# A selective-scan block kernel: GpSimd makes six of sixteen drive units, the opening is cut in halves, and the last sum is taken in HBM

## The chip, the cores and the metric

The kernel runs on one NeuronCore of a Trainium2 chip. The metric is the device time of one execution in microseconds (us), the median of several runs; lower is better. One execution was also recorded by the hardware profiler, and all rows below come from that one.

## What is computed

For 16 sequences of 256 tokens with 128 features the reference computes two residual blocks:

```python
x = x + layernorm(block(layernorm(x)))          # block: a gated selective scan (state space model)
x = x + layernorm(ffn(layernorm(x)))            # ffn: both operands rounded to fp8 e4m3, one 128x128 product, bias
# inside block, with 256 inner channels and 16 states each:
xz = x @ W_in + b_in; x_in, z = split(xz)
xc = silu(causal_conv4(x_in) + conv_b)
B, C = split(xc @ W_xp + b_xp); delta = softplus(xc @ W_dt + b_dt)
h[t] = exp(delta[t] * A) * h[t-1] + (delta[t] * xc[t]) * B[t]      # per channel and state
y = sum over states of h * C + D_skip * xc
out = (y * silu(z)) @ W_out + b_out; returns norm(x + out) * alpha + beta
```

The second term of the recurrence, delta * xc * B, is called the drive here, and delta * xc is `u`.

## The kernel before, in words

**Tiling.** Sequences are worked on in eight pairs. In a pair the 256 channels are two halves of 128 partitions, and the 16 states are eight groups of two (`SG = 2`). A unit is one group of one sequence of the pair, so a pair has sixteen units, numbered n = 2 * group + sequence, and each unit has two scans (one per half of the channels) of 128 partitions by 512 elements: two states of 256 steps.

**A unit's way.** The drive of a unit is made by TensorE (PE) in `drive_unit`: `uT`, the transposed `u`, is multiplied by `diag`, a matrix that has B on its diagonal, so that PSUM then holds u times B for two states (four matmuls in the program for a unit, eight records in the trace). `diag` is made by GpSimd (POOL) in `diag_b` with one affine select (L500), and there are four buffers of it. ScalarE (ACT) makes `decay`, exp(delta * A), in `exp_decay` (L745). VectorE (DVE) runs the scan in `scan_half` (L1200), with decay from SBUF and the drive from PSUM. PE transposes the states back (L1011), and they are scaled by C and summed over the groups: for five groups ACT scales (L766) and a DMA issued by POOL adds the result up in SBUF (`add_terms`, L516), for the groups in `DIRECT = (3, 6, 7)` DVE does both (`add_direct`, L1223).

**Slots.** The work is software-pipelined by hand. In slot p the sixteen units of pair p run; beside them the front of pair p+1 (projections, silu, softplus, `u`, B and C) and the back of pair p-1 (sum of the states in `sum_states` L525 and L527, gate, output product, three norms). Every engine runs `slot()` over its own list of instructions in order. The dictionaries `POOL_STEPS`, `ACT_STEPS`, `PE_STEPS` and `DVE_STEPS` say after which step of a slot a piece of front or back work is issued; POOL and DVE count two steps per unit, PE and ACT three. `LEAD = 3` says how many units POOL's `diag` is ahead. The drive has two PSUM buffers of two banks, the states have four buffers. Slots 1 to 6 are a loop; slot 0 has no back, slot 7 no front.

**Opening.** Before slot 0 the front of pair 0 is done in a line: load, layer norm, transposition (L924), `w_tap` = W_in times the convolution weights (L1397), input product (L938 to L943), bias into `pre` (L688) and then silu (L696), the delta product (L954), softplus as exp and log (L722, L726), `delta` (L1189), `u` on POOL (L488), its transposition (L978) and copy (L731), and the first drive.

**Tail.** After slot 7 comes the back of pair 7, then the largest absolute value of all, then the ffn for eight groups of 512 tokens: ACT scales (L864), DVE and POOL round to fp8 (L1462, L1465, L626, L1473), PE multiplies (L1140, L1144), DVE takes statistics (L1482), ACT normalizes into `fn` (L872), POOL adds the residual `x_all` into `fo` (`last_sum`, L633), and the SP queue stores it (L449).

**Queues.** SP issues the loads in a fixed order at the start (L424 to L443) and only the eight stores at the end. POOL issues the 64 accumulating DMAs.

## Time and profile before

| What | us |
|---|---|
| median of 3 runs (lowest, highest) | 639.04 (636.86, 639.94) |
| the profiled execution | 639.14 |
| its span, from the first record to the last | 637.4 |
| PE busy | 542.6 (85%) |
| DVE busy | 504.8 (79%) |
| ACT busy | 441.9 (69%) |
| POOL busy | 300.7 (47%) |

The profiled execution took 1.74 us more than its span. The stretches that the prediction speaks of are: opening 0 to 43.6, slot 0 43.6 to 108.3, slots 1 to 6 up to 505.0 (the one at 240.7 to 306.3 is shown), slot 7 up to 566.5, the back of the last pair up to 593.8, and the tail to 637.4. A busy share is a mean over all of these, and the engine with the largest share need not set the pace in each.

### The profile page before, as it was taken

The page shows a single profiled execution, that of the slowest core. Times are in us where ns is not written, and L with a number is a line of the kernel's source. Part 1 is how long each engine was busy: PE and PEld are TensorE (multiplying, and loading weights), DVE is VectorE, ACT ScalarE, POOL GpSimd, SP SyncE. Part 2 cuts the span into 40 slices and gives each one's busy share as a digit, 9 for nine tenths or more (in the row PEclk, how much of TensorE's full clock was granted, in tenths as well). Part 3 has the DMA queues.
Part 4 walks back from the last instruction along what each step waited for, and adds up shares of the span by engine and source line. Part 5 has one row for each costly group of instructions (what it writes and reads, how often), then busy time and mean ns, then how long its engine had stood idle before and what let it go on. Part 6 is the DMA issues. An engine that isn't in the chain of part 4 may idle for free. (4 is left out here: it accounts for less than half of the span.)

```text
span 637.4 us, 10358 instructions
## 1 busy us (share of the span) xinstructions
PE 542.6 (85%) x2893; PEld 419.1 (66%) x2893; DVE 504.8 (79%) x1001; ACT 441.9 (69%) x885; POOL 300.7 (47%) x333
## 2 busy tenths in 40 slices
PE   4979899999899988998999899998999797861571
PEld 3557687787678866876687767786778686660120
DVE  4036698979887988799979878888989989974695
ACT  2466985799659874989498938894799586702364
POOL 2042343656455563458255826373647465401374
PEclk9979999999899999999999999999999999977555
DMA  7000535053502460155115420624052506510012
GB/s 209 22 1 1 100 67 100 1 100 66 101 2 55 79 134 1 33 99 107 25 33 99 87 47 9 123 46 86 1 112 54 99 10 124 106 27 0 1 51 82
DMA packets 19184, 39.84 MB, mean 62 GB/s; under 512 B 3648, under 2 KB 9920, under 8 KB 19136
## 3 DMA queue, kind: packets, MB, share of 16 engines
q0 software_dynamic: 9216, 33.56, 26.7%
q1 hardware_dynamic: 9920, 5.78, 3.3%
q14 instruction: 35, 0.29, 0.1%
q8 instruction: 13, 0.21, 0.1%
HBM read 3.68 MB, written 2.10 MB: 9 GB/s over the span
## 5 line engine op out<-in xcount | busy, mean ns | idle before, releaser
L1200 DVE TENSOR_TENSOR_SCAN state<-decay,drive 128x512 f32<-128x512 f32 x256 | 297.2, 1203 | 30.7 <-PE drive L995 24.9
L995 PE MATMUL drive<-diag,uT 128*128 128x256 f32 x1024 | 245.9, 384 | 0.7 <-ACT uT L731 0.7
L745 ACT ACTIVATE decay<-delta,a_neg 128x510 f32<-128x510 f32 x256 | 170.5, 730 | 54.8 <-DVE state L1200 53.9
L995 PEld LDWEIGHTS drive<-diag,uT 128*128 128x128 f32 x1024 | 187.1, 193 | 21.7 <-ACT uT L731 1.0
L1011 PE MATMUL hT<-ident,state 128*128 128x128 f32 x1024 | 143.0, 278 | 24.3 <-DVE acc_d L1223 19.1
L1011 PEld LDWEIGHTS hT<-ident,state 128*128 128x128 f32 x1024 | 119.8, 143 | 56.3 <-issue 26.1
L500 POOL TENSOR_SCALAR_AFFINE_SELECT diag<-Bt 128x512 f32<-128x512 f32 x128 | 92.1, 725 | 74.5 <-PE drive L995 58.2
L766 ACT ACTIVATE term<-hT,Ct 128x256 f32<-128x256 f32 x256 | 102.9, 484 | 8.8 <-PE hT L1011 8.8
L516 POOL DMA_DIRECT2D acc<-term x64 | 59.9, 935 | 24.1 <-DMA acc<-term 11.8
L1223 DVE SCALAR_TENSOR_TENSOR acc_d<-hT,Ct,acc_d 128x256 f32<-128x256 f32 x160 | 66.5, 470 | 4.4 <-PE hT L1011 4.3
L938 PE MATMUL fbank<-xnT,w_tap 128*128 128x512 f32 x112 | 50.4, 592 | 0.0
L552 POOL TENSOR_TENSOR bstd<-bvar,half 128x4 f32<-128x4 f32 x8 | 8.3, 1032 | 62.3 <-DVE bvar L1270 62.3
L938 PEld LDWEIGHTS fbank<-xnT,w_tap 128*128 128x128 f32 x112 | 21.5, 192 | 21.1 <-issue 20.2
L472 POOL TENSOR_TENSOR rstd<-var,minus_half 128x4 f32<-128x4 f32 x9 | 9.3, 1031 | 52.8 <-DVE var L1161 52.8
L656 ACT ACTIVATE nrm<-res,bshift,bscale 128x128 f32<-128x128 f32 x32 | 13.1, 481 | 25.9 <-DVE bshift L1254 25.9
L954 PE MATMUL fbank<-xc,w_dt 128*128 128x512 f32 x60 | 28.3, 594 | 0.7 <-ACT xc L696 0.7
L766 ACT ACTIVATE acc<-hT,Ct 128x256 f32<-128x256 f32 x64 | 25.1, 485 | 4.0 <-PE hT L1011 4.0
L552 POOL TENSOR_TENSOR bstd<-bvar,minus_half 128x4 f32<-128x4 f32 x16 | 16.5, 1029 | 24.2 <-DVE bvar L1292 14.9
L525 POOL TENSOR_TENSOR ysumT<-acc 128x512 f32<-128x512 f32 x14 | 17.8, 1270 | 20.8 <-DVE acc_d L1223 20.8
L688 ACT ACTIVATE pre<-fbank,in_bias 128x512 f32<-128x512 f32 x14 | 9.6, 688 | 23.5 <-PE fbank L941 23.5
L532 POOL TENSOR_TENSOR yv<-yv,sz 128x1024 f32<-128x1024 f32 x7 | 16.5, 2360 | 15.2 <-DVE yv L1229 15.2
L488 POOL TENSOR_TENSOR u<-delta,xc 128x1024 f32<-128x1024 f32 x8 | 18.8, 2350 | 7.8 <-DVE delta L1189 7.8
(170 smaller groups left out, 624.9 us busy)
## 6 DMA issues: line engine op xcount, KB each, us to landing
acc<-term POOLq DMA_DIRECT2D x64, 512.0 KB, 4.5
out_dram<-state SPq DMA_DIRECT2D x8, 256.0 KB, 2.2
x_all<-in_L_attn_x_dram SPq DMA_DIRECT2D x2, 256.0 KB, 4.2
state<-in_L_attn_conv_w_dram SPq DMA_DIRECT2D x1, 512.0 KB, 5.4
w_in<-in_L_attn_W_in_dram SPq DMA_DIRECT2D x1, 256.0 KB, 3.2
w_dt<-in_L_attn_W_dt_dram SPq DMA_DIRECT2D x1, 256.0 KB, 5.1
w_out<-in_L_attn_W_out_dram SPq DMA_DIRECT2D x1, 128.0 KB, 3.8
w_ffn<-in_L_ffn_weight_dram SPq DMA_DIRECT2D x1, 64.0 KB, 2.4
```

What stands on the lines that cost most here:

```text
L488: nc.gpsimd.tensor_tensor(u[:, :, :], d, xc[:, par, :, :], ALU.mult).then_inc(u_ready, 1)
L500: nc.gpsimd.affine_select(out=diag[:, n % DIAGS, :, :, :].rearrange("p c s t -> p (c s) t"), in_=b_cols, compare_op=ALU.is_equal, fill=0.0 ...
L516: pool.dma_start(acc[:, par, b, :, :, :], term[:, j % TERMS, :, :, :], accum_op=ALU.add)\
L552: nc.gpsimd.tensor_tensor(bstd[:, :], bvar[:, :], (half if k == 0 else minus_half)[:, :], ALU.pow)\
L745: last = nc.scalar.activation(decay[:, g % DECAYS, h, :, s, 1:], delta[:, par, h, :, 1:], ACT.Exp, scale=a_neg[:, h, SG * g + s:SG * g + s ...
L766: last = nc.scalar.activation(into, hT[:, c, DI * s:DI * s + DI], ACT.Copy, scale=Ct[:, par, TC * b + c, SG * g + s:SG * g + s + 1])
L938: nc.tensor.matmul(front_bank(pr, k), w_tap[:, tap, P * k:P * k + P], xnT[:, :, tap:tap + L], start=(tap == 0), stop=False)
L954: last = nc.tensor.matmul(front_bank(pr, 4 + m), w_dt[:, h, P * m:P * m + P], xc[:, par, h, :], start=(h == 0), stop=(h == HALVES - 1))
L995: last = nc.tensor.matmul(dst[:, :, P * c:P * c + P], uT[:, par, TC * b + c, P * h:P * h + P], diag[:, n % DIAGS, c, :, :], start=True, st ...
L1011: last = nc.tensor.transpose(hT[:, c, DI * s + P * h:DI * s + P * h + P], state[:, n % STATES, h, s, P * c:P * c + P], ident[:, :])
L1200: nc.vector.tensor_tensor_scan(state[:, n % STATES, h, :, :].rearrange("p s t -> p (s t)"), decay[:, g % DECAYS, h, b, :, :].rearrange("p ...
L1223: nc.vector.scalar_tensor_tensor(out=a, in0=src, scalar=by, in1=a, op0=ALU.mult, op1=ALU.add)\
```

## The change

**Drive.** For groups `MADE = (1, 3, 5)`, that is units 2, 3, 6, 7, 10 and 11, `drive_unit` and `diag_b` do nothing on PE. Instead POOL multiplies u by B in SBUF (`make_drive`, two instructions of 128x512 per unit) into the buffer `made`, and the scan of these units reads both inputs from SBUF. For this B must stand in all 128 partitions: SP stores B of the three groups to an internal HBM tensor `b_rows`, element by element, and loads each group back as a broadcast row of 4 KB to every partition into `b_all`, which has one buffer, so the load of the second and third group waits until the group before is used up. **Buffers.** `diag` has two buffers instead of four, and LEAD is 2. `pre` shares the space of `dt_v`, and the sum of the states is taken in place in `acc`.

**Places.** Most entries of the step dictionaries move.

**Opening.** `w_tap` is made ahead of the quantization of the ffn weight, with its load issued earlier; silu reads PSUM directly; exp, log, delta and `u` are done in halves; `u` of pair 0 and one of the two copies of `uT` go to DVE; the norm of pair 1 moves ahead on ACT.

**Tail.** SP stores x after the first block (`store_x1`) to the output in each slot, and the normalized ffn result is added to it in HBM by an accumulating DMA that POOL issues. `fn` has four buffers, and `last_sum` and `fo` are gone.

```diff
-LEAD = 3
+LEAD = 2
 DECAY_LEAD = 1
-DECAYS, DIAGS, STATES, TERMS = 2, 4, 4, 4
+DECAYS, DIAGS, STATES, TERMS = 2, 2, 4, 4
...
+MADE = (1, 3, 5)
+DRIVEN_G = tuple(g for g in range(DS // SG) if g not in MADE)
+DRIVEN = PAIR * len(DRIVEN_G)
+MADES = PAIR * HALVES * len(MADE)
...
-POOL_STEPS = dict(front_root=(3,), front_residual=(24,), front_u=(25,), back_gate=(11,), back_affine=(21,),
-                  back_sum=(25,), sum_states=(6,), back_root=(13, 22, 27))
-ACT_STEPS = dict(back_h2T=(47,), front_xin=(8, 9), silu_table=(21,), front_silu=(21, 22, 23), exp_table=(23,),
-                 front_norm=(14,), front_xnT=(23,), front_dt=(29, 30), front_exp=(35,), front_log=(37,),
-                 front_uT=(42, 46), back_norms=(32, 40, 45))
-PE_STEPS = dict(front_in=(0, 6, 15, 21), front_transpose=(23,), front_dt=(24, 28), front_bc=(37,),
-                front_ut=(40, 41), back_y=(12, 14), back_out=(19,), back_transpose=(45,))
-DVE_STEPS = dict(front_stats=(1,), front_shift=(1,), front_low=(19,), front_bc=(25,), front_delta=(24,),
-                 back_y=(8, 9), back_norms=(12, 13, 17, 21, 24, 27, 27), back_amax=(31,))
+POOL_STEPS = dict(front_root=(2,), front_residual=(31,), front_u=(26,), back_gate=(10,), back_affine=(19,),
+                  back_sum=(25,), sum_states=(6,), back_root=(15, 21, 26))
+ACT_STEPS = dict(back_h2T=(46,), front_xin=(6, 9), silu_table=(21,), front_silu=(21, 22, 23), exp_table=(23,),
+                 front_norm=(7,), front_xnT=(23,), front_dt=(27, 30), front_exp=(35,), front_log=(37,),
+                 front_uT=(45, 46), back_norms=(31, 39, 46))
+PE_STEPS = dict(front_in=(0, 6, 12, 21), front_transpose=(23,), front_dt=(24, 28), front_bc=(33,),
+                front_ut=(42, 42), back_y=(13, 15), back_out=(19,), back_transpose=(45,))
+DVE_STEPS = dict(front_stats=(0,), front_shift=(2,), front_low=(19,), front_bc=(23,), front_delta=(23,),
+                 back_y=(8, 9), back_norms=(12, 13, 17, 21, 23, 27, 27), back_amax=(31,))
...
+        b_rows = nc.dram_tensor("b_rows", [len(MADE), PAIR * TC * SG, P], F32, kind="Internal").ap()
+        b_all = sb("b_all", [P, PAIR, TC, SG, P])
+        made = sb("made", [P, PAIR, HALVES, SG, L])
...
+            def spread_b(pr, par):
+                sp.wait_ge(bc_ready, nth(pr, 3, 2))
...
+                for k, g in enumerate(MADE):
...
+                    sp.dma_start(b_rows[k].rearrange("r p -> p r"),
+                                 Bt[:, par, g, :, :, :].rearrange("p b c s -> p (b c s)"), **slow).then_inc(b_stored[k], 16)
+                for k, g in enumerate(MADE):
+                    sp.wait_ge(b_stored[k], nth(pr, 16, 16))
...
+                    if k:
+                        sp.wait_ge(made_ready, nth(pr, MADES, PAIR * HALVES * k))
...
+                    sp.dma_start(b_all[:, :, :, :, :].rearrange("p b c s t -> p (b c s t)"),
+                                 b_rows[k].rearrange("(o r) p -> o (r p)", o=1).to_broadcast([P, SG * TOK]))\
+                        .then_inc(b_spread[k], 16)
...
+            def store_x1(pr):
+                sp.wait_ge(b_sum, nth(pr, 1, 1))
...
+                sp.dma_start(out_v[:, bass.ds(pr.v * CH, CH), :], x_k[:, bass.ds(pr.v * CH, CH), :]).then_inc(x1_stored, 16)
...
+            def make_drive(pr, par, n):
+                g, b = n // PAIR, n % PAIR
+                j, k = turn(MADE, n), MADE.index(g)
+                pool.wait_ge(u_ready, nth(pr, 1, 1))
+                pool.wait_ge(b_spread[k], nth(pr, 16, 16))
+                old = trailing(pr, par, j, PAIR, PAIR * len(MADE))
+                if old:
+                    pool.wait_ge(scan_done, nth(old[0], 2 * UNITS, 2 * unit(MADE, old[2]) + 2))
+                for h in range(HALVES):
+                    u_h = u[:, h, L * b:L * b + L].rearrange("p (c t) -> p c t", c=TC).unsqueeze(1).to_broadcast([P, SG, TC, P])
+                    nc.gpsimd.tensor_tensor(made[:, b, h, :, :].rearrange("p s (c t) -> p s c t", c=TC), u_h,
+                                            b_all[:, b, :, :, :].rearrange("p c s t -> p s c t"), ALU.mult).then_inc(made_ready, 1)
...
             def diag_b(pr, par, n):
                 g, b = n // PAIR, n % PAIR
-                if n == 0:
+                if g in MADE:
+                    make_drive(pr, par, n)
+                    return
+                m = turn(DRIVEN_G, n)
+                if m == 0:
...
-            def last_sum(grp, par):
+            def add_to_out(grp, par):
                 pool.wait_ge(f_norm, nth(grp, 1, 1))
-                if grp.after(2):
-                    pool.wait_ge(stored[par], (grp.v - par) * 8)
-                nc.gpsimd.tensor_tensor(fo[:, par, :], fn[:, par, :], x_all[:, bass.ds(grp.v * TOK, TOK)], ALU.add)\
-                    .then_inc(f_out, 1)
+                pool.dma_start(out_v[:, CH * grp.v:CH * grp.v + CH, :], chunks(fn[:, grp.v % 4, :]), accum_op=ALU.add)\
+                    .then_inc(stored[grp.v % 4], 16)
             def tail(grp, par):
                 old, new = other(grp, par, -3), other(grp, par, 1)
-                if old:
-                    last_sum(*old)
                 if new:
                     round_up(*new)
+                if old:
+                    if old[0].v == 0:
+                        pool.wait_ge(x1_stored, 16 * PAIRS)
+                    add_to_out(*old)
...
-            act.wait_ge(w_in_loaded, 16 * 2)
+            front_norm(Pair(1), 1)
...
             for h in range(HALVES):
-                front_xin(Pair(0), h)
+                act.wait_ge(front_full, 1 + h)
+                nc.scalar.activation(xc[:, 0, h, :], front_bank(Pair(0), h), ACT.Silu, bias=in_bias[:, h:h + 1])\
+                    .then_inc(xin_ready, 1)
...
+            for h in range(HALVES):
+                act.wait_ge((half_low, dt_low)[h], 1)
+                nc.scalar.activation(dt_e[:, h, :], dt_e[:, h, :], ACT.Exp).then_inc((half_exp, sp_exp)[h], 1)
+            for h in range(HALVES):
+                act.wait_ge((half_exp, sp_exp)[h], 1)
+                nc.scalar.activation(dt_e[:, h, :], dt_e[:, h, :], ACT.Ln, bias=1.0).then_inc((half_log, sp_log)[h], 1)
+            act.wait_ge(a_neg_ready, 1)
+            exp_decay(Pair(0), 0, 0)
+            front_uT(Pair(0), 0, 0)
...
-                b = n % PAIR
-                if n == 0:
+                g, b = n // PAIR, n % PAIR
+                if g in MADE:
+                    return
+                m = turn(DRIVEN_G, n)
+                if m == 0:
                     pe.wait_ge(uT_ready, nth(pr, 2, 2))
-                pe.wait_ge(diag_ready, nth(pr, UNITS, n + 1))
-                old = trailing(pr, par, n, 2)
+                pe.wait_ge(diag_ready, nth(pr, DRIVEN, m + 1))
+                old = trailing(pr, par, m, 2, DRIVEN)
...
-                dve.wait_ge(drive_ready, nth(pr, 2 * UNITS, 2 * n + h + 1))
+                if g in MADE:
+                    dve.wait_ge(made_ready, nth(pr, MADES, HALVES * turn(MADE, n) + h + 1))
+                    new = made[:, b, h, :, :].rearrange("p s t -> p (s t)")
+                else:
+                    m = turn(DRIVEN_G, n)
+                    dve.wait_ge(drive_ready, nth(pr, 2 * DRIVEN, 2 * m + h + 1))
+                    new = drive[:, m % 2, h, :]
                 nc.vector.tensor_tensor_scan(state[:, n % STATES, h, :, :].rearrange("p s t -> p (s t)"),
                                              decay[:, g % DECAYS, h, b, :, :].rearrange("p s t -> p (s t)"),
-                                             drive[:, n % 2, h, :], 0.0, ALU.mult, ALU.add).then_inc(scan_done, 1)
+                                             new, 0.0, ALU.mult, ALU.add).then_inc(scan_done, 1)
...
+            dve.wait_ge(w_in_loaded, 16)
+            dve.wait_ge(tap_loaded, 16)
+            for tap in range(TAPS):
+                nc.vector.tensor_tensor(w_tap[:, tap, :], w_in[:, 0:DI], cw_r[:, :, tap], ALU.mult).then_inc(taps_ready, 1)
+            dve.wait_ge(x_second, 16)
+            front_stats(Pair(1))
...
+            d = delta[:, 0, :, :, :].rearrange("p h b t -> p h (b t)")
+            for h in range(HALVES):
+                dve.wait_ge((half_log, sp_log)[h], 1)
+                nc.vector.tensor_tensor(d[:, h, :], dt_v[:, h, :], dt_e[:, h, :], ALU.max)\
+                    .then_inc((half_delta, delta_ready)[h], 1)
+                dve.wait_ge((half_delta, delta_ready)[h], 1)
+                nc.vector.tensor_tensor(u[:, h, :], d[:, h, :], xc[:, 0, h, :], ALU.mult).then_inc((half_u, u_ready)[h], 1)
+            dve.wait_ge(front_full, 9)
+            nc.vector.tensor_copy(uT[:, 0, 2:4, :], front_bank(Pair(0), 8).rearrange("p (j d) -> p j d", d=DI))\
+                .then_inc(uT_ready, 1)
```

## Rows read from the trace of the kernel before

**Rows 1.** Windows: from:to, length, busy us of each engine, PEclk, DMA share, GB/s.
```profile
0.00:43.60 43.60, 30.50 (x116) 20.32 (x117) 10.05 (x43) 20.10 (x32) 11.17 (x28) 0.94 0.32 85
43.60:108.30 64.70, 62.71 (x323) 48.02 (x323) 49.53 (x66) 47.77 (x92) 22.47 (x28) 0.99 0.33 66
...
240.70:306.30 65.60, 60.39 (x339) 48.16 (x338) 57.62 (x108) 52.21 (x103) 35.72 (x38) 1.00 0.33 64
...
505.00:566.50 61.50, 48.72 (x290) 41.91 (x290) 55.37 (x99) 35.69 (x77) 28.00 (x30) 0.95 0.35 69
...
593.80:637.40 43.60, 21.17 (x51) 6.90 (x49) 31.74 (x108) 20.48 (x56) 21.71 (x16) 0.50 0.16 49
```

**Rows 2.** Windows, the middle of the slot of 240.7 to 306.3, same columns.
```profile
262.00:290.00 28.00, 27.51 (x165) 22.57 (x163) 23.56 (x46) 25.72 (x48) 15.29 (x18) 1.00 0.38 75
```

**Rows 3.** Waits of DVE in the same slot: total us, times, longest.
```profile
DVE res L1264 <- PE bbank L1029: 1.9, 1, 1.9
DVE shift L1165 <- POOL rstd L472: 1.2, 1, 1.2
```

**Rows 4.** Groups of instructions by line, whole span: busy us, mean ns, idle before.
```profile
L1200 DVE TENSOR_TENSOR_SCAN state<-decay,drive 128x512 f32<-128x512 f32 x256 | 297.2, 1203 | 30.7 <-PE drive L995 24.9 <-ACT decay L745 5.0 <-PE hT L1011 0.9
L995 PE MATMUL drive<-diag,uT 128*128 128x256 f32 x1024 | 245.9, 384 | 0.7 <-ACT uT L731 0.7
...
L500 POOL TENSOR_SCALAR_AFFINE_SELECT diag<-Bt 128x512 f32<-128x512 f32 x128 | 92.1, 725 | 74.5 <-PE drive L995 58.2 <-DVE Ct L1182 16.3
...
L516 POOL DMA_DIRECT2D acc<-term x64 | 59.9, 935 | 24.1 <-DMA acc<-term 11.8 <-issue 6.5 <-ACT term L766 5.9
...
L525 POOL TENSOR_TENSOR ysumT<-acc 128x512 f32<-128x512 f32 x14 | 17.8, 1270 | 20.8 <-DVE acc_d L1223 20.8
```

**Rows 5.** One line, L1165: duration ns least/median/greatest, first and last start.
```profile
L1165 DVE SCALAR_TENSOR_TENSOR shift<-mv,rstd x9: 155/595/598, 6.3 to 446.0; 128x4 f32<-128x4 f32 x9
```

**Rows 6.** Timeline of DVE and POOL: start, us, engine, line, operation [idle before].
```profile
251.65 5.65 DVE L1200 TENSOR_TENSOR_SCAN state<-decay,drive 128x512 f32<-128x512 f32 x5
...
251.90 1.27 POOL L525 TENSOR_TENSOR ysumT<-acc 128x512 f32<-128x512 f32 x1 [3.39 <-DVE acc_d L1223]
```

**Rows 7.** DMA issues: queue, operation, count, KB each, median us to landing.
```profile
acc<-term POOLq DMA_DIRECT2D x64, 512.0 KB, 4.5
out_dram<-state SPq DMA_DIRECT2D x8, 256.0 KB, 2.2
...
state<-in_L_attn_conv_w_dram SPq DMA_DIRECT2D x1, 512.0 KB, 5.4
...
bin_c<-in_L_attn_b_in_dram SPq DMA_DIRECT2D x1, 2.0 KB, 3.0
```

**Rows 8.** Timeline of the opening.
```profile
13.85 5.52 PE L938 MATMUL drive<-xnT,w_tap 128*128 128x512 f32 x8 [4.33 <-DVE w_tap L1397]
...
25.59 1.05 ACT L696 ACTIVATE xc<-pre 128x1024 f32<-128x1024 f32 x1
...
32.18 1.65 ACT L656 ACTIVATE xn<-x_all,shift,rstd 128x128 f32<-128x128 f32 x4 [1.00 <-DVE shift L1165]
...
37.20 2.35 POOL L488 TENSOR_TENSOR u<-delta,xc 128x1024 f32<-128x1024 f32 x1 [1.48 <-DVE delta L1189]
...
43.64 1.22 DVE L1200 TENSOR_TENSOR_SCAN state<-decay,drive 128x512 f32<-128x512 f32 x1 [6.53 <-PE drive L995]
```

**Rows 9.** Timeline of the tail, DVE, then POOL.
```profile
602.51 0.42 DVE L1462 TENSOR_SCALAR state<-state 128x512 int32<-128x512 int32 x1
...
605.44 0.42 DVE L1462 TENSOR_SCALAR state<-state 128x512 int32<-128x512 int32 x1
...
608.37 1.50 DVE L1462 TENSOR_SCALAR state<-state 128x512 int32<-128x512 int32 x1
...
612.38 1.49 DVE L1462 TENSOR_SCALAR state<-state 128x512 int32<-128x512 int32 x1
...
608.01 1.57 POOL L633 TENSOR_TENSOR state<-term,x_all 128x512 f32<-128x512 f32 x1 [0.28 <-ACT term L872]
```

More of the change, by code:

```diff
@@ L132, in turn, with unit @@
     return PAIR * groups.index(n // PAIR) + n % PAIR
+def unit(groups, j):
+    return PAIR * groups[j // PAIR] + j % PAIR
 def directs(j, s, c):
@@ L198, in build_sandwich @@
         dt_v = sb("dt_v", [P, HALVES, TOK])
+        pre = dt_v
         dt_e = sb("dt_e", [P, HALVES, TOK])
@@ L308, in build_sandwich @@
         drive_ready = sem("drive_ready")
+        made_ready = sem("made_ready")
+        sp_waited = sem("sp_waited")
+        b_stored = [sem("b_stored_%d" % k) for k in range(len(MADE))]
+        b_spread = [sem("b_spread_%d" % k) for k in range(len(MADE))]
         scan_done = sem("scan_done")
@@ L354, in build_sandwich @@
         f_norm = sem("f_norm")
-        f_out = sem("f_out")
-        stored = [sem("stored_even"), sem("stored_odd")]
+        x1_stored = sem("x1_stored")
+        stored = [sem("added_%d" % k) for k in range(4)]
         x_v = x.rearrange("b l d -> (b l) d").rearrange("(k p) d -> p k d", p=P)
@@ new lines, in store_x1 @@
+            def store_x1(pr):
+                sp.wait_ge(b_sum, nth(pr, 1, 1))
+                sp.sem_inc(sp_waited, 1)
+                sp.dma_start(out_v[:, bass.ds(pr.v * CH, CH), :], x_k[:, bass.ds(pr.v * CH, CH), :]).then_inc(x1_stored, 16)
+            spread_b(Pair(0), 0)
+            with sp.Fori(0, (PAIRS - 2) // 2) as i:
+                for k in range(2):
+                    pr = Pair(i * 2 + (1 + k), 1 + k)
+                    spread_b(pr, 1 - k)
+                    store_x1(pr.plus(-1))
@@ L454, in _ @@
+            spread_b(Pair(PAIRS - 1), 1)
+            store_x1(Pair(PAIRS - 2))
+            store_x1(Pair(PAIRS - 1))
+            sp.wait_ge(x1_stored, 16 * PAIRS)
+            for k in range(4):
+                sp.wait_ge(stored[k], 16 * PAIRS // 4)
         @block.gpsimd
@@ L522, in sum_states @@
                 for b in range(PAIR):
-                    total = ysumT[:, TC * b:TC * b + TC, :]
+                    total = acc[:, par, b, :, 0, :]
                     pool.wait_ge(sum_done[b], nth(pr, 16 * ADDS, 16 * ADDS))
-                    nc.gpsimd.tensor_tensor(total, acc[:, par, b, :, 0, :], acc[:, par, b, :, 1, :], ALU.add).then_inc(ysum_part, 1)
+                    nc.gpsimd.tensor_tensor(total, total, acc[:, par, b, :, 1, :], ALU.add).then_inc(ysum_part, 1)
                     pool.wait_ge(ysum_part, nth(pr, PAIR, b + 1))
@@ L610, in _ @@
             front_residual(Pair(0), 0)
-            front_u(Pair(0), 0)
             slot(Pair(0), 0, True, False)
@@ L1020, in back_y @@
                 for j in range(CH):
-                    last = nc.tensor.transpose(back_bank(pr, h)[:, P * j:P * j + P], ysumT[:, j, P * h:P * h + P], ident[:, :])
+                    last = nc.tensor.transpose(back_bank(pr, h)[:, P * j:P * j + P], acc[:, par, j // TC, j % TC, 0, P * h:P * h + P], ident[:, :])
                 last.then_inc(back_full, 1)
@@ L1421, in _ @@
             for b in range(PAIR):
-                total = ysumT[:, TC * b:TC * b + TC, :]
+                total = acc[:, 1, b, :, 0, :]
                 dve.wait_ge(sum_done[b], nth(last_pair, 16 * ADDS, 16 * ADDS))
-                nc.vector.tensor_tensor(total, acc[:, 1, b, :, 0, :], acc[:, 1, b, :, 1, :], ALU.add).then_inc(ysum_part, 1)
+                nc.vector.tensor_tensor(total, total, acc[:, 1, b, :, 1, :], ALU.add).then_inc(ysum_part, 1)
                 dve.wait_ge(ysum_part, nth(last_pair, PAIR, b + 1))
```

127 lines of the change are left out of this document (69 added, 58 removed).

## The prediction

> **What bounds the kernel now.** I read the windows by stage first, because the shares of the whole page mix an opening, eight slots and a tail. In a looped slot of about 66 us PE is busy 60.4 us and DVE 57.6 us of 65.6 [rows 1]: both are near the end, and POOL has 30 us free. The windows inside this slot then show where PE leads: from 262 to 290 PE is busy 27.5 of 28 us while DVE has 4.4 us idle [rows 2]; outside that stretch DVE is as full as PE. The waits of DVE give the rest of its 8.0 us idle: 1.9 for the output product, 1.2 for POOL's root that nothing covers [rows 3]. So whatever PE is spared, a slot can shrink by those 8 us at most, and then DVE sets the pace. Slot 7 has PE at 48.7 of 61.5 and DVE at 55.4: DVE leads there already. Slot 0 is the reverse, PE 62.7 of 64.7 and DVE 49.5 [rows 1].
>
> **Removed from PE.** A unit's drive is 8 of the 1,024 records of L995, 245.9 / 128 = 1.9 us [rows 4]; six units are 11.5 us a slot. PE falls to about 49 of 65.6 and leads nowhere. PE is then idle a quarter of the slot; slot 7, busy to 79%, was granted 0.95 in the mean [rows 1], so I cost the clock at nothing.
>
> **Added to POOL.** Twelve products of 128x512 a slot. The nearest row is a POOL tensor_tensor of the same size, 1.27 us [rows 4]: 15.2 us. Six affine selects go, 6 x 0.73 = 4.4. POOL comes to 35.7 + 15.2 - 4.4 = 46.5 busy of 65: not the bound by itself.
>
> **What the scans pay.** A scan is 1.20 us [rows 4], at first assumed equal when both inputs are in SBUF, since the recurrence, 2.3 ns an element, is slower than any plain operation of DVE here. But the trace shows DVE and POOL shutting each other out. `shift`, a four-element operation with two SBUF inputs, takes 0.155 us at best and 0.595 at the median, when it starts beside POOL's affine select [rows 5]. In the tail L1462 takes 0.42 us alone and 1.50 when POOL's L633 runs, and L633 itself takes 1.57 instead of 1.27 [rows 9, 4]. Today's scans don't suffer: five of them take 5.65 us beside POOL's four sums [rows 6], and their drive comes from PSUM. A made scan has two SBUF inputs, so I take it to wait as `shift` does. Low end: no wait, if a scan is no such operation. High end: each of 12 waits for a whole POOL instruction, 15.2 us a slot. Between: POOL's instructions that touch SBUF are 46.5 less 8 DMA issues of 0.94 [rows 4], about 39 of 65 us, 0.6. Met at a random place the wait is half of 1.27: 12 x 0.6 x 0.64 = 4.6 us. I take 5.0 with the small operations. The Trainium skill (SBUF — State Buffer, Who interferes with whom) states it as a rule: a DVE instruction with two SBUF inputs contends with a GpSimd one that reads SBUF, and the second to issue blocks until the first has finished. By that rule the low end is out, and the first rival gives the sum.
>
> **Slots 1 to 6.** DVE busy 57.6, plus 5.0, plus the idle that stays: 8.0 less 4.4 (PE's stretch) less 1.2 (stats and shift are now two steps apart, a scan between them) = 2.4. That makes 65.0 against 65.6, or -0.6; the slot shown is the shortest and the others are 66.2, with the same DVE work, so -0.9 each: -5.4.
>
> **B through HBM.** SP issues three stores of 1,024 elements of 4 bytes and three broadcast loads of 512 KB a slot. The load's twin is the broadcast of the convolution weights, 5.4 us to landing; the store's nearest is `bin_c`, 512 scattered elements, 3.0 us; between 3 and twice that [rows 7]. B is ready at step 23 of a slot, but SP must first see the block sum (POOL step 25) to store x1: step 26 of 32 leaves 6/32 of 65.6, 12 us, to the slot's end. Issues, 3.0 and 5.4 us need 9 to 12 us, so POOL may stand 0 to 2 us at its first product; the scan that needs it comes 11 us after the slot starts (240.7 to 251.65, [rows 1, 6]), so DVE is covered. Behind that wait on POOL's queue stand the second product and the root for `shift`; cost 0 to 2 us a slot, taken as 0 because the scan is covered, the rest in the range. The second and third loads wait for the buffer; POOL has two driven units, some 8 us, to cover 6. `diag` with two buffers holds POOL to PE's pace in units 12 to 15 only; PE is early then: 0. The DMA share was 0.33 [rows 1]; three loads more are bearable: 0. In-place sums and `pre`: same work, 0. The Trainium skill (DMA: Bandwidth & Descriptors, its rules for kernel authors) says that a strided last dimension becomes one descriptor per element; it gives no time for it, and the sum doesn't use it.
>
> **Slot 0.** DVE 49.5 + 4 (fewer POOL instructions) + 4 (B of pair 0 lands some 10 us after it is computed and POOL, with the root behind, waits) + 2.5 idle = 60 against 64.7: -4.7; ends -10 and +3. **Slot 7.** DVE 55.4 + 4.6 + 4.5 of its 6.1 idle = 64.5 against 61.5: +3; ends -3 and +8.
>
> **Opening** [rows 8]. First product at 13.85, waiting for `w_tap`; with its 5.4 us load [rows 7] issued fourth instead of seventh and 2.2 us of work, about 10.4: -3.4. Silu from PSUM takes its 1.05 us and the bias step off the way to the delta product, which then waits for PE's own products: -1.8. The norm of 1.65 us in front of exp goes: -1.7. `u` on DVE in halves under log instead of 2.35 on POOL: -1.4. Transpose and copies of `uT` in halves: -0.8. Half instructions' fixed cost: +0.2. Sum -8.9; ends -5 and -11.
>
> **Back of pair 7:** the same. **Tail.** Groups come every 2.93 us (602.51 to 605.44) until L633 is there, then every 4.01 [rows 9]; without L633 four steps save 4.3. The end has POOL's DMA issue and an accumulating landing, between 2.2 and 4.5 us [rows 7], instead of sum, issue and 2.2: +1. The issue has 512 rows where `acc` had 128; 0.9 us or up to four times that: +0 to +5, taken nearest the known row, since other groups hide it. -3.5; ends -5 and +5.
>
> **Sum.** -8.9 - 4.7 - 5.4 + 3 + 0 - 3.5 = -19.5 on the profiled 639.1 (span 637.4 and 1.7 around it): 619.6. The median lies 0.1 lower: 619.5.
>
> **Rivals.** *Alternation (slower).* Where POOL waits when a scan ends, it takes the next turn and the next scan waits for it. That happens for sure at units 2 and 3: POOL's four sums start 0.25 us after the scans [rows 6], so three scans wait 1.27 = 3.8 us. The other eight wait 0.6 x 1.2 = 0.7 each, 5.7. Lock cost 9.5 instead of 4.6: slots 1 to 6 +4.9, or +29; slots 0 and 7 +3 and +3; total 619.5 + 35 = 654.5. It decides above about 7.3 us a slot, 0.6 per made scan. For it: L1462's turns in the tail, one after the other. Against: some waits fall into idle. 0.28 with the neighbouring mishap that B comes late (+5 a slot on six slots, 650). *No lock.* The scan takes its operands as it does now: minus 5.0 x 6, 4 and 4.6: 581. Against it are rows 5 and 9, which however show no scan. 0.12. *Given back in the slots.* POOL at 46.5 plus its own blocked time and ACT at 52 of 65 pass waits to each other and the slots grow by 3: only opening and tail remain and a part of them is eaten, 635.8 to 642.2: 0.12. That the change doesn't do what it says: the six units' products are plainly gone from PE, no chance given.
>
> **Numbers.** Forecast's case 0.48 (own range 600 to 635). A measurement of this kernel tells 0.5%, 3.2 us, from no change. Faster: 0.48 + 0.12 = 0.60; same 0.12; slower 0.28. The range 590 to 656 leaves out most of "no lock" and the upper part of "alternation".
>
> **What would show it.** L995 x640 instead of x1024; first scan near 35 us; PE near 49 us busy in a looped slot. Made scans with a mean of 1.2 (no lock), 1.6 (forecast) or 2.0 us (alternation), and POOL products above 1.27. DVE's waits for `made` or POOL's for `b_all` above 3 us a slot would make the lock the wrong story. Tail groups 2.9 us apart. A first scan later than 39 us would make the opening wrong.

## The result: 760.8 us, slower by 19%

The changed kernel takes 760.77 us (median of 4 runs, 755.67 to 764.05) against 637.95 for the kernel before beside it (635.31 to 639.94): a ratio of 1.190, interval 1.185 to 1.195. The forecast was 619.5, and its range ended at 656. The profiled execution has a span of 758.2 us against 637.4.

First the windows of the changed kernel, to be held against [rows 1]: the opening, the looped slot from one issue of B's stores to the next, the tail. Columns as there.

```profile
0.00:36.30 36.30, 28.67 (x106) 18.08 (x107) 14.12 (x49) 16.89 (x29) 8.87 (x25) 0.94 0.49 102
344.70:427.10 82.40, 58.86 (x299) 45.02 (x298) 64.99 (x109) 53.01 (x105) 54.30 (x45) 0.88 0.52 74
718.60:758.20 39.60, 20.66 (x48) 6.72 (x48) 23.68 (x104) 20.47 (x56) 20.32 (x16) 0.50 0.52 53
```

The opening is 36.3 us instead of 43.6, the tail 39.6 instead of 42.0 (595.45 to 637.4). The slots, with the back of the last pair, are the loss: 758.2 - 36.3 - 39.6 = 682.3 us where they had 551.8, so +130.5. The slot shown is like the others: from one issue of B's stores to the next they take 82.1 to 84.7 us. In it PE is busy 59 of 82 us and DVE 65. No engine is full; something makes all of them wait.

Groups of instructions by line, forms apart, whole span; then the page's line of the same kind for PE. Answers to [rows 4].

```profile
L1299 DVE TENSOR_TENSOR_SCAN state<-decay,drive 128x512 f32<-128x512 f32 x160 | 187.0, 1203 | 37.8 <-issue 22.1 <-PE drive L1076 14.5 <-remote 0.3
L1299 DVE TENSOR_TENSOR_SCAN state<-decay,made 128x512 f32<-128x512 f32 x96 | 147.1, 1574 | 7.7 <-POOL made L556 7.6
L1374 DVE TENSOR_SCALAR bstd<-bstd 128x4 f32<-128x4 f32 x8 | 14.3, 1793 | 1.2 <-POOL bstd L625 1.2
L556 POOL TENSOR_TENSOR made<-u,b_all 128x512 f32<-128x512 f32 x96 | 126.9, 1368 | 35.0 <-DMA b_all<-b_rows 29.8 <-DVE state L1299 3.6 <-issue 1.6
L598 POOL TENSOR_TENSOR acc<-acc 128x512 f32<-128x512 f32 x14 | 27.8, 1984 | 13.7 <-DVE acc_d L1322 13.7
```
```profile
L1076 PE MATMUL drive<-diag,uT 128*128 128x256 f32 x640 | 170.5, 415 | 16.1 <-POOL diag L573 15.3
```

The same line of code gives 1.203 us for a scan whose drive comes from PSUM and 1.574 in the mean for one whose drive is `made` in SBUF. The shortest of the 96 took 1.19 and half of them at most 1.28, the longest 2.29: a drive in SBUF is not slow by itself, some of the scans are held. And POOL's sums, 1.27 us before [rows 4], now take 1.98: both sides pay. The drives are x640, as foreseen.

The waits of the whole span (total, times, longest):

```profile
DVE shift L1258 <- POOL rstd L527: 63.9, 8, 14.1
POOL acc L589 <- issue: 108.8, 10, 16.6
POOL made L556 <- DMA b_all<-b_rows: 29.8, 7, 21.5
SPq L478 <- DMA b_rows<-Bt: 66.9, 12, 11.9
```

L589 is POOL's issue of an accumulating transfer; it waits in program order for the transfer before it into the part of `acc` that belongs to the same sequence. "issue" says only that no instruction was found as the releaser; before, this wait was 6.5 us in all [rows 4]. The timeline of one slot, SP's queue and then POOL, and the landing times of L589 over the span (a landing is the end of a transfer) tell what it waited for:

```profile
344.74 1.70 SPq L474 DMA_DIRECT2D b_rows<-Bt  x3
355.64 37.27 SPq L485 DMA_DIRECT2D b_all<-b_rows  x3
...
347.73 0.91 POOL L589 DMA_DIRECT2D acc<-term  x1
...
349.00 1.16 POOL L589 DMA_DIRECT2D acc<-term  x1
350.62 0.62 POOL L573 TENSOR_SCALAR_AFFINE_SELECT diag<-Bt 128x512 f32<-128x512 f32 x1 [0.46 <-PE drive L1076]
366.94 0.87 POOL L589 DMA_DIRECT2D acc<-term  x1 [15.70 <-issue]
367.52 1.58 POOL L536 TENSOR_TENSOR xnb<-xn,bout_r 128x512 f32<-128x512 f32 x1
369.72 4.92 POOL L556 TENSOR_TENSOR made<-u,b_all 128x512 f32<-128x512 f32 x4 [0.61 <-DMA b_all<-b_rows]
374.60 1.03 POOL L527 TENSOR_TENSOR rstd<-var,minus_half 128x4 f32<-128x4 f32 x1
```
```profile
DMA to landing us min/median/max: 4.4/4.5/21.6
```

Three stores of B are issued at 344.7. Accumulating transfers are issued at 347.7 and 349.0, and the next issue stands until 366.9. Over the span such a transfer took up to 21.6 us to land instead of 4.5; before, the longest took 6.5. POOL stands 15.7 us here, and 14.6 to 16.6 at the same place of five other slots, with the products and the root behind it; B itself lands 0.6 us after POOL gets to it. The windows show what happens meanwhile (columns as above). Right behind the stores the DMA engines are busy 97% of the time and move only 16 GB/s, where the whole slot has 74. Later everything stops, PE has no instruction from 369 to 374, and the clock goes to its lower level, 1.2 GHz, just as the work comes back.

```profile
349.00:354.00 5.00, 4.27 (x26) 3.67 (x25) 5.00 (x8) 3.76 (x8) 1.78 (x3) 1.00 0.97 16
...
364.00:369.00 5.00, 2.04 (x7) 0.94 (x5) 0.00 (x0) 0.00 (x0) 2.06 (x2) 1.00 0.90 189
369.00:374.00 5.00, 0.00 (x0) 0.00 (x0) 0.00 (x0) 0.00 (x0) 4.39 (x5) 0.57 0.43 85
374.00:379.00 5.00, 0.40 (x2) 0.40 (x3) 3.33 (x7) 2.61 (x6) 2.83 (x4) 0.50 0.33 107
```

### The profile page after: what moved, and what is told of

Same layout as the page of the kernel before. It is cut to its first block, busy times and chain, and to the rows that moved or that the text cites. A ratio compares the mean times of both kernels' runs of the same rounds, so it can differ in the third digit from the quotient of the medians.

```text
span 758.2 us, 9756 instructions
## 1 busy us (share of the span) xinstructions
PE 518.5 (68%) x2499; PEld 386.9 (51%) x2499; DVE 552.3 (73%) x1007; ACT 442.0 (58%) x884; POOL 443.0 (58%) x380
## 2 busy tenths in 40 slices
DMA packets 51825, 54.61 MB, mean 72 GB/s; under 512 B 29120, under 2 KB 39488, under 8 KB 51776
## 4 chain that ended last, share of the span: by engine, by line
DMA 22%; POOL 20%; DVE 20%; issue 17%; PE 13%; ACT 5%; SPq 1%; DVEq 1%; POOLq 1%; ACTq 0%
DMA b_all<-b_rows 14%; POOL made L556 8%; DMA b_rows<-Bt 8%; DVE state L1299 7%; POOL acc L598 4%; PE hT L1092 3%; PE drive L1076 3%; DVE acc_d L1322 2%; POOL acc L600 2%; PE bbank L1110 2%; POOL yv L605 2%; DVE bstd L1374 2%; ACT nrm L727 1%; DVE bst L1342 1%; PE drive L1014 1%
## 5 line engine op out<-in xcount | busy, mean ns | idle before, releaser
L1092 PE MATMUL hT<-ident,state 128*128 128x128 f32 x1024 | 168.6, 309 | 144.3 <-DVE acc_d L1322 111.2
L1092 PEld LDWEIGHTS hT<-ident,state 128*128 128x128 f32 x1024 | 135.7, 161 | 184.9 <-DVE acc_d L1322 99.9
L1299 DVE TENSOR_TENSOR_SCAN state<-decay,drive 128x512 f32<-128x512 f32 x160 | 187.0, 1203 | 37.8 <-issue 22.1
L816 ACT ACTIVATE decay<-delta,a_neg 128x510 f32<-128x510 f32 x256 | 169.5, 721 | 55.3 <-issue 31.4
L1076 PE MATMUL drive<-diag,uT 128*128 128x256 f32 x640 | 170.5, 415 | 16.1 <-POOL diag L573 15.3
L1299 DVE TENSOR_TENSOR_SCAN state<-decay,made 128x512 f32<-128x512 f32 x96 | 147.1, 1574 | 7.7 <-POOL made L556 7.6
L556 POOL TENSOR_TENSOR made<-u,b_all 128x512 f32<-128x512 f32 x96 | 126.9, 1368 | 35.0 <-DMA b_all<-b_rows 29.8
L1076 PEld LDWEIGHTS drive<-diag,uT 128*128 128x128 f32 x640 | 128.8, 212 | 35.0 <-POOL diag L573 12.3
L589 POOL DMA_DIRECT2D acc<-term x64 | 62.9, 988 | 112.6 <-issue 108.8
L573 POOL TENSOR_SCALAR_AFFINE_SELECT diag<-Bt 128x512 f32<-128x512 f32 x80 | 71.5, 899 | 33.3 <-PE drive L1076 18.4
L727 ACT ACTIVATE xn<-x_all,shift,rstd 128x128 f32 (+1 forms) x36 | 14.8, 481 | 100.2 <-DVE shift L1258 100.2
L598 POOL TENSOR_TENSOR acc<-acc 128x512 f32<-128x512 f32 x14 | 27.8, 1984 | 13.7 <-DVE acc_d L1322 13.7
L625 POOL TENSOR_TENSOR bstd<-bvar,half 128x4 f32<-128x4 f32 x8 | 14.8, 1846 | 33.5 <-DVE bvar L1369 33.5
L600 POOL TENSOR_TENSOR acc<-acc,acc_d 128x512 f32<-128x512 f32 x14 | 27.3, 1949 | 1.1
```

What stands on the lines that cost most here:

```text
L556: nc.gpsimd.tensor_tensor(made[:, b, h, :, :].rearrange("p s (c t) -> p s c t", c=TC), u_h, b_all[:, b, :, :, :].rearrange("p c s t -> p s ...
L573: nc.gpsimd.affine_select(out=diag[:, m % DIAGS, :, :, :].rearrange("p c s t -> p (c s) t"), in_=b_cols, compare_op=ALU.is_equal, fill=0.0 ...
L589: pool.dma_start(acc[:, par, b, :, :, :], term[:, j % TERMS, :, :, :], accum_op=ALU.add)\
L598: nc.gpsimd.tensor_tensor(total, total, acc[:, par, b, :, 1, :], ALU.add).then_inc(ysum_part, 1)
L600: nc.gpsimd.tensor_tensor(total, total, acc_d[:, par, b, :, :], ALU.add).then_inc(ysum_ready, 1)
L816: last = nc.scalar.activation(decay[:, g % DECAYS, h, :, s, 1:], delta[:, par, h, :, 1:], ACT.Exp, scale=a_neg[:, h, SG * g + s:SG * g + s ...
```

## The experiments

Two theories stood at the start. S: the scattered stores of B hold the DMA engines, so B and the accumulating transfers come late. L: DVE and POOL shut each other out (the lock of the prediction), and POOL's long queue of instructions in order does the rest. Each run was timed beside the kernel before, which had medians of 639.5, 638.4, 639.5 and 639.9 in the four groups of four.

**B in rows of 32 bytes.** `b_rows` and `b_all` keep time outside, so a store has 128 rows of 32 bytes instead of 1,024 pieces of 4; the products read `b_all` with a stride of 8 elements.

```diff
-b_rows = nc.dram_tensor("b_rows", [len(MADE), PAIR * TC * SG, P], F32, kind="Internal").ap()
+b_rows = nc.dram_tensor("b_rows", [len(MADE), P, PAIR * TC * SG], F32, kind="Internal").ap()
```

> The changed kernel with B stored to HBM in rows of 32 bytes (128 pieces a store instead of 1,024 of 4 bytes); GpSimd reads b_all with a stride of 8 elements. Theory S (the scattered stores hold the DMA engines for some 20 us a slot, so B and the accumulating transfers come late): first load of a slot lands in about 4 us instead of 13.9, VectorE's waits for the root behind the first products (63.9 us) go nearly to zero, slots of 66 to 68 us, total 625 to 650. Theory L (the lock between VectorE and GpSimd, and GpSimd's queue, make the slots long): total stays above 710. If GpSimd's strided reading is slow, products rise above 1.27 us and the total lies between.

Measured 685.1 us, ratio 1.073 (1.068 to 1.078): between the two. The DMA issues, of this kernel:

```profile
b_rows<-Bt SPq DMA_DIRECT2D x24, 4.0 KB, 2.1
```

The store lands in 2.1 us and 76 us are back, but the products, strided now, went from a median of 1.27 to 1.75 us, and 46 us over the kernel before remain. POOL stands 23.6 us in all at the accumulating transfers. Both theories hold a part.

**Each store followed by its own load.** The first loop over `MADE` no longer ends before the second begins.

```diff
                     sp.dma_start(b_rows[k].rearrange("r p -> p r"),
                                  Bt[:, par, g, :, :, :].rearrange("p b c s -> p (b c s)"), **slow).then_inc(b_stored[k], 16)
-                for k, g in enumerate(MADE):
                     sp.wait_ge(b_stored[k], nth(pr, 16, 16))
```

> The changed kernel with each group's store followed by its own load, so that the second and third store stand behind the first load. Theory S: the first B comes some 10 us sooner and the wait at the first product shrinks, but the later loads and the accumulating transfers are still slowed: 690 to 740. If the lateness were a fixed cost of a store (one round trip to HBM), nothing changes: 750 to 765. Theory L: 750 to 765.

Measured 678.4 us, in one single execution. The same kernel again, in the last group of runs:

> The kernel in which each store of B is followed by its own load, timed again for an interval: 676 to 682, ratio 1.06 to 1.07.

Measured 691.7 us (median of four, 690.2 to 693.6), ratio 1.082 (1.077 to 1.087), outside what was expected and 13 us more than the one execution of the first time, while the kernel before moved by 0.4. Why is open, so small steps around this kernel can't be read. The large one can: the order of six DMA issues is worth 69 to 82 us. The issues, of the first of the two runs:

```profile
b_rows<-Bt SPq DMA_DIRECT2D x24, 4.0 KB, 10.9
```

One store of 1,024 pieces takes 10.9 us to land. In the changed kernel the load issued at 355.64, when the first store had landed, comes to POOL only at 369.7: with the other two stores still under way it takes 14 us instead of its median of 3.7, and the accumulating transfers are as late. Here POOL waited 31.4 us in all at the same issue, instead of 108.8, and the longest landing of an accumulating transfer was 10.6 us.

**No made units.** `MADE = ()`; two diag buffers, lead, places, opening and tail stay changed.

> The changed kernel with MADE empty: all sixteen drives on TensorE, no B through HBM, but LEAD and two diag buffers, the new places, the opening and the tail stay. All theories that put the loss on the six units: 639 less 7.3 (first scan at 36.3 instead of 43.6) less about 4 in the tail, so 622 to 634. If places or two diag buffers cost by themselves: above 640.

Measured 657.2 us, ratio 1.030 (1.024 to 1.037). POOL's waits show why; before it was 58.2 [rows 4].

```profile
POOL diag L573 <- PE drive L1076: 210.3, 73, 6.8
```

**The stores alone**, added to the kernel before, with nobody reading them: `sp.dma_start(b_rows[k]...)` three times a slot (and a wait of DVE before it writes over B, at which its list of waits shows none).

> The kernel before with only the three scattered stores of B issued in each slot; nothing reads them. Theory S with its second path (stores delay the accumulating transfers, and GpSimd waits for those in order): landings of the accumulating transfers near 20 us for one or two of eight a slot, total 660 to 710. If the loss comes only through the wait for B itself: 637 to 643. Theory L: 637 to 643.

Measured 666.0 us, ratio 1.043 (1.039 to 1.047). Waits of POOL:

```profile
POOL acc L536 <- issue: 87.0, 9, 12.9
```

The longest landing of an accumulating transfer is 16.1 us here. So the stores hurt where nothing needs their data, by 26.5 us, through the accumulating transfers: POOL's wait rose from 6.5 to 87.0 us.

**B spread once.** Stores and loads for pair 0 and one group only; the products stay. It leaves out the right B.

```diff
+                if pr.after(1):
+                    return
...
-                pool.wait_ge(b_spread[k], nth(pr, 16, 16))
+                pool.wait_ge(b_spread[0], 16)
```

> B is stored and spread once, for pair 0 and the first made group; all later products read those values, so the traffic of B is gone and nothing else. Leaves out the right B. Theory S (the scattered stores and what they hold up are the loss; the lock is worth 4.5 us a slot): 620 to 645, products 1.27 us, made scans 1.5 to 1.6 us in the mean. Theory L (lock and the order of POOL's queue are a loss of their own, as the 73.7 us slot with 32-byte rows hints): 655 to 685, with POOL's sums at 2.0 us and DVE waiting for POOL's products or for its drive over 5 us a slot.

Measured 666.9 us, ratio 1.044 (1.039 to 1.048): without any of B's traffic the design still loses 28 us. Theory S alone is out.

**No products.** The scans read what was made once; POOL's products are left out.

```diff
+                if pr.after(1) or n // PAIR != MADE[0]:
+                    return
                 for h in range(HALVES):
```

> As with B spread once, and POOL makes its products only for the first made group of pair 0; all later scans of the six units read those. Leaves out the drives of the six units. The scans still have two SBUF inputs, but POOL has 15.2 us a slot less. If the products (their lock and their place in POOL's queue) are what costs beyond the traffic: 585 to 610, near DVE's own 57.6 us a slot, made scans 1.2 to 1.35 us. If a scan from SBUF is slow by itself, or two diag buffers hold the slot: 620 or more.

Measured 652.7 us, ratio 1.023 (1.017 to 1.030). Groups of this kernel, a scan and POOL's sum:

```profile
L1292 DVE TENSOR_TENSOR_SCAN state<-decay,made 128x512 f32<-128x512 f32 x96 | 149.5, 1600 | 0.0
...
L591 POOL TENSOR_TENSOR acc<-acc 128x512 f32<-128x512 f32 x14 | 29.6, 2112 | 29.9 <-DVE acc_d L1315 29.9
```

The scans are as slow as ever, 1.600 us, though POOL has 108 us less to do (333.5 against 441.8 with B spread once). What holds them is not the products but POOL's old work in the same places. The timeline shows the turns they take with two of POOL's sums:

```profile
247.36 7.65 DVE L1292 TENSOR_TENSOR_SCAN state<-decay,made 128x512 f32<-128x512 f32 x4
...
247.62 2.02 POOL L591 TENSOR_TENSOR acc<-acc 128x512 f32<-128x512 f32 x1 [4.43 <-DVE acc_d L1315]
249.72 2.07 POOL L593 TENSOR_TENSOR acc<-acc,acc_d 128x512 f32<-128x512 f32 x1
```

Four scans take 7.65 us where four of 1.20 take 4.8, so 2.9 us of the 4.8 that the twelve scans of a slot lose are lost here.

**Four diag buffers, lead of three**, again without made units; then also the old places, so that only opening and tail differ from the kernel before.

```diff
-LEAD = 2
+LEAD = 3
-DECAYS, DIAGS, STATES, TERMS = 2, 2, 4, 4
+DECAYS, DIAGS, STATES, TERMS = 2, 4, 4, 4
```

> As the kernel without made units, but with four diag buffers and a lead of three, as before; places, opening and tail stay those of the changed kernel. If the two diag buffers were its loss: 626 to 634 (before, less 7 in the opening and 2.4 in the tail), and POOL's wait for PE's drive back at some 60 us. If the new places cost by themselves: 645 or more.

> Before's slots (all drives on PE, four diag buffers, before's places) with the changed kernel's opening and tail alone. Both theories: 639 less 7.3 (first scan 36.3 instead of 43.6) less 2.4 (tail 39.6 instead of 42) = 629, 625 to 633. Should it be above 636, the opening's gain is eaten in slot 0.

Measured 635.2 us (ratio 0.996, 0.993 to 0.998) and 634.3 us (0.992, 0.989 to 0.996). Two buffers with a lead of two cost 22 us while PE makes all sixteen drives; buffers and lead were changed together. The new places cost nothing that can be told (1 us). The second is a version that beats both kernels, by 0.8%. It gains 4 to 5 us and not the 9.7 of opening and tail, and came out above the 625 to 633 that was expected: the six stretches from one group of `front_stats` to the next take 66.9 us each in the mean against 66.2 before, which accounts for 4.4. Not slot 0 (63.3 in both) but the looped slots grew; no run shows why.

**PE kept busy.** PE repeats half of each driven unit's products, with the same result; once on "no products", once on the kernel of the store order.

```diff
-                    for c in range(TC):
+                    for c in (0, 1, 0, 1) if h == 0 else (0, 1):
```

> As the kernel without products, but PE repeats half of each driven unit's products (four more of eight, 40 more a slot, same result), so that PE has 9.6 us a slot more to do at 2.4 GHz. Clock theory (PE, spared 11.5 us a slot, idles, its clock falls to 1.2 GHz for parts of the slot, and the transposes and drives then run at half speed on the path): granted clock back above 0.93 and 625 to 640 us instead of 652.7. If the clock costs nothing and the lock on the scans is all: 650 to 665.

> The changed kernel with each store of B followed by its own load, and PE repeating half of each driven unit's products. Clock theory: 678 less 10 to 20 = 658 to 668, granted clock above 0.92. Lock and traffic theory: 672 to 685.

Measured 672.1 us and 706.9 us, slower by 19.4 and by 15 to 28.5. The granted clock was 0.896 and 0.892; without the repeats it had been 0.893, and 0.869 and 0.852, so it rose little. As a test of the clock this failed; what it shows is that time added to the drives costs although PE has some 9 of 70 us left in a slot (61.4 busy of 70.35). What the clock itself costs stays open.

**Scans from PSUM.** As "no products", but the six units' scans read the bank of the driven unit before, and PE overwrites that bank after the last of them.

```diff
-                    new = made[:, b, h, :, :].rearrange("p s t -> p (s t)")
+                    new = drive[:, turn(DRIVEN_G, PAIR * g - 1) % 2, h, :]
```

> As the kernel without products, but the scans of the six units read a PSUM bank (the drive of the unit before) instead of made, so that they have one SBUF input. Leaves out the drives of the six units. Lock theory: scans back to 1.20 us in the mean (from 1.60), DVE near 500 us busy, and the time down by most of 36 us: 615 to 630. Clock theory alone: the lock is partly covered, 635 to 650, with the granted clock at or below 0.89.

> Both together: scans from PSUM and PE kept busy. If lock and clock are two separate losses: 590 to 612, DVE's own 57.6 us a slot plus little. If one of them covers the other: no lower than the lower one of the two single runs less 5 us.

Measured 617.1 us (ratio 0.965, 0.961 to 0.969) and, with PE's repeats, 650.6. One operand moved from SBUF to PSUM takes 35.6 us away (652.7 to 617.1), all 256 scans have a mean of 1.203 us, and POOL's sums are back at 1.275: the lock, priced by itself, for both engines together. PE waits longer for its bank in this run, so the price is rather low than high.

**Five diag buffers.** The same with `b_all` and `made` left out and their space used; the drives of the six units are left out as in the two kernels before.

> As the kernel whose scans read PSUM (617 us), with b_all and made left out and in their space five diag buffers instead of two, and a lead of three. Leaves out the drives of the six units. Two-buffer theory (22 us were lost to two buffers when PE made all sixteen drives): 590 to 605. If ten drives fit through two buffers and the waits of the round trip are the bound: 612 to 619, and the forecast's 2.4 us of idle DVE in a slot was wrong by itself.

Measured 615.4 us, ratio 0.961 (0.956 to 0.966). Its looped slot, and its groups for scan and sum:

```profile
227.00:291.20 64.20, 51.87 (x278) 38.52 (x279) 56.85 (x108) 51.40 (x102) 32.06 (x32) 0.97 0.35 70
```
```profile
L1271 DVE TENSOR_TENSOR_SCAN state<-decay,drive 128x512 f32<-128x512 f32 x256 | 296.4, 1203 | 24.1 <-PE drive L1049 16.1 <-PE hT L1065 7.0
...
L568 POOL TENSOR_TENSOR acc<-acc 128x512 f32<-128x512 f32 x14 | 17.8, 1274 | 38.2 <-DVE acc_d L1294 38.2
```

With ten drives two buffers cost 1.7 us, not 22, and even that is within the two intervals (0.956 to 0.966 against 0.961 to 0.969). And the slot still has 7.4 us in which DVE is idle (64.2 less 56.85), and its neighbour 9.5 (66.13 less 56.66), against 8.0 before. Scan and sum are both at 1.20 and 1.27.

**Loads alone.** The three loads stay in every slot, the stores are made for pair 0 only.

> The changed kernel with the three stores for pair 0 only; the three loads of 512 KB stay in every slot. Leaves out the right B after pair 0. Theory: the loads are bearable, 665 to 673, within 5 us of the kernel that spreads B once (667). If the loads and not the stores hold the accumulating transfers: 685 or more.

Measured 676.9 us, ratio 1.057 (1.050 to 1.064): the loads cost 10 us, more than the 5 expected. But they do not hold the accumulating transfers, whose longest landing is 7.0 us; POOL's wait in this kernel:

```profile
POOL acc L586 <- issue: 16.0, 10, 3.3
```

With the 16.1 us and 87.0 us of the stores alone, this leaves the stores as what holds them.

**Products later.** `MADE = (2, 3, 5)` in the changed kernel, one line.

> The changed kernel with MADE = (2, 3, 5) instead of (1, 3, 5): the first product comes two units, some 8 us, later in POOL's order, and the root for shift is no longer behind it. If B's lateness is the loss (82 us in eight slots by the order of stores and loads): 690 to 725, with shift's wait for the root from 63.9 us to under 15. If it is the held accumulating transfers (landing up to 21.6 us), which do not depend on when B is used: 745 or more.

Measured 767.4 us, ratio 1.202 (1.196 to 1.207). Waits of this kernel:

```profile
DVE shift L1258 <- POOL rstd L527: 24.2, 6, 7.4
POOL acc L589 <- issue: 103.1, 11, 15.3
```

`shift` waits 40 us less, POOL's wait for B falls from 29.8 to 10.1, and no time is gained: POOL still stands 103 us at the accumulating transfers. In the changed kernel both ways are about equally long (B lands 0.6 us after POOL gets to it), and the chain that ended last goes through B's loads and stores for 13.8% and 7.7% of the span; here these are 3.7% and 3.0%. So B late at its first product is not the loss by itself: relieving it alone leaves POOL at the transfers that the same stores hold.

**The whole, step by step**, medians in us; most steps are one edit, and the kernels are the ones above. They come from different groups of runs, so steps of 1 or 2 us are not told from nothing:

| step | time | difference |
|---|---|---|
| kernel before | 639 | |
| new opening and tail | 634.3 | -5 |
| new places | 635.2 | +1 |
| six units off PE, scans from PSUM, enough diag buffers | 615.4 | -20 |
| two diag buffers, lead of two | 617.1 | +2 |
| the six scans read SBUF | 652.7 | +36 |
| POOL makes the products | 666.9 | +14 |
| three loads of 512 KB a slot | 676.9 | +10 |
| three stores of 1,024 pieces, each before its load | 678.4, 691.7 | +2 to +15 |
| the three stores ahead of the loads | 760.8 | +69 to +82 |

## Why the prediction was wrong, by its own steps

The forecast was 619.5 and the result 760.8, 141 us apart. By the runs above some 90 of them are B's traffic (94 measured, 4 written, in slot 0), some 40 are the case without lock and traffic (577 by the prediction's terms, 617 measured), and 11 are the lock with POOL's products (38.6 written, 49.9 measured).

**Opening and tail: right, but half of it did not reach the total.** First scan at 36.33 against 43.64 [rows 8], -7.3 where -8.9 was written. Tail -2.4 where -3.5 was; groups came every 2.93 us, as said, and POOL's issue into the output took 1.3 us and landed in 5.1. In the kernel with these two parts alone 4 to 5 of the 9.7 us were left, because its looped slots were longer. Timelines of POOL in the tail and of DVE in the opening:

```profile
726.74 1.26 POOL L697 TENSOR_TENSOR state<-state 128x512 f32<-128x512 f32 x1 [1.67 <-DVE state L1578]
729.67 1.26 POOL L697 TENSOR_TENSOR state<-state 128x512 f32<-128x512 f32 x1 [1.67 <-DVE state L1578]
...
733.80 1.34 POOL L702 DMA_DIRECT2D out_dram<-term  x1
```
```profile
36.33 1.22 DVE L1299 TENSOR_TENSOR_SCAN state<-decay,drive 128x512 f32<-128x512 f32 x1 [2.27 <-PE drive L1076]
...
57.68 0.58 DVE L1258 SCALAR_TENSOR_TENSOR shift<-mv,rstd 128x4 f32<-128x4 f32 x1 [13.59 <-POOL rstd L527]
```

The second line is slot 0: B of pair 0 came 21.5 us late to POOL, and slot 0 took 72.8 us from one `front_stats` to the next, against 63.3; written were some 10 us of lateness and a slot 0 shorter by 4.7. Slots 1 to 6 were written as 65.0 to 65.3 us and are 82.1 to 84.7.

**"Three loads more are bearable: 0" and "B through HBM ... POOL may stand 0 to 2 us": the step that failed.** It costs 94 us (666.9 to 760.8) of the 122 between the two kernels. Three things were wrong in it. The store was priced between 3.0 and 6 us from `bin_c`, 512 pieces; 1,024 took 10.9 and 11.4. The three stores were taken as if the first load could follow the first store, while the code issues all three first. And, the largest, the step asked only when B arrives. It did not ask what else is under way on the DMA engines just then: the accumulating transfers of the last units, for which POOL waits in order. The share of 0.33 [rows 1] is a mean over the slot and says nothing of the 20 us behind the stores, which begin with 5 us at 0.97. The Trainium skill (DMA: Bandwidth & Descriptors, its rules for kernel authors) says that a strided last dimension lowers to one descriptor per element and should be rearranged; the trace agrees, 29,120 packets under 512 bytes against 3,648 before, and the same bytes in rows of 32 landed in 2.1 us. The prediction named this and its sum did not use it; the range should have reached further there.

**"Plus the idle that stays: 8.0 less 4.4": wrong.** PE busy to the brim from 262 to 290 [rows 2] was read as PE holding DVE up for 4.4 us. With six units gone and no lock at all (five diag buffers), DVE still idles 7.4 us in a slot. Its waits there, over the span, are 16.1 us for drives, 14.8 and 11.0 for the output products and 7.0 for transposes, with PE busy 52 of 64 us. It waits for PE's answers while PE is not full: from 241 to 248 DVE is busy 4.7 us and PE 6.45 of 7. Whether PE's round trips alone make this, or ACT, busy 51 of 64, has a part in it, is not separated. The case "no lock" was put at 581; the nearest run, which has no products either, took 617.

**The lock: right in size by luck, wrong in kind.** Written: 4.6 us a slot; measured: the 96 scans of the changed kernel take 35.6 us more than at 1.203 each, and the run with scans from PSUM gave 35.6 us of time, both 4.5 a slot. The rule of the Trainium skill (SBUF — State Buffer, Who interferes with whom) that a DVE instruction with two SBUF inputs and a GpSimd one that reads SBUF contend with each other holds for a scan too: 1.57 us in the mean with both inputs in SBUF, 1.20 with one. But it was worked out as scans met by POOL at random for 0.6 of the time; the run without products gives the same 1.60 us, and the timeline shows the turns beside the four sums that the rival *Alternation* described. That rival's mechanism was right for units 2 and 3, with 2.9 us a slot instead of its 3.8; for the other eight scans it wrote 5.7 where under 2 are left, so its total was too high. What POOL itself pays, 1.27 to 2.11 us a sum, stood in no term.

**"I take 5.0 with the small operations": too little.** POOL's products cost 14.3 us beyond the lock on scans, 1.8 a slot instead of 0.4. Between these two kernels DVE's busy time rises by 17.7 us (536.2 to 553.9), and 13 of them are one four-element operation right behind POOL's root, the one that L1374 shows above: 1.8 us in the mean, 0.16 before.

**"`diag` with two buffers ...: 0": right here**, 1.7 us and within the noise, though with the lead of two it would be 22 with all drives on PE.

**"I cost the clock at nothing": open.** The slot is granted 0.88 in the mean, where it had 1.00. The windows show it down right behind stretches in which PE had little or nothing to do. A record of the drives takes 415 ns in the mean instead of 384 [rows 4], 20 us more of PE's time over the 640. How much of the loss the clock makes no run separates.

Of the cases, that in which B comes late had the right place and a price of 5 us a slot; measured is 11.7 for the traffic alone (94 / 8).

## What to carry to other kernels

Before a transfer is called hidden, list what else the same DMA engines carry in that stretch and who waits for it, and count pieces, not bytes: a mean share over a slot does not show it. An engine that is full in a window need not be the bound; look whether the others wait for its capacity or for its answer. When two waits end within a microsecond of each other, relieving one of them shows nothing. Moving an operand from PSUM to SBUF can cost more than the instruction that it saves, on both engines, and what decides is what POOL already does beside it.

## What the runs showed of the hardware that was not expected

- Scattered stores slow what stands beside them: with three of 1,024 pieces of 4 bytes just issued, accumulating transfers landed in up to 21.6 us, where the median is 4.5 and the longest before was 6.5. The DMA engines were then busy 97% of the time and moved 16 GB/s.
- The order of DMA issues alone, same bytes and pieces, moved the kernel from 678 or 692 to 761 us.
- A DVE operation of four elements with one tensor as input took 1.8 us in the mean beside POOL's products and 0.16 without them. The Trainium skill (SBUF — State Buffer, Who interferes with whom) lists `tensor_scalar` among the operations that can take the port pair shared with GpSimd, when its operands meet certain conditions. The trace fits that; whether this one met them no run shows. The prediction had looked only at two-input operations.
- The lock costs a scan the same whether POOL has 442 or 334 us of work: 1.58 and 1.60 us.
